# Ten unread TensorE products in the wait before the expert layer's first reload

## The chip, the cores and the metric

The kernel runs on one core of a Trainium2 chip. The metric is the device time of one execution in microseconds (us); lower is better. TensorE (PE) multiplies, VectorE (DVE) and ScalarE (ACT) do element-wise work, GpSimd (POOL) makes constants and scatters rows, and SyncE (SP) issues most DMAs. TensorE's clock has two levels here, 2.4 GHz (granted clock 1.00) and 1.2 GHz (0.50).

## The reference, cut to what matters

```python
def reference(x, ...):
    x = _L0_conv_ref(x, ...)           # group norm, deformable attention, GEGLU
    t = _to_tokens(x)                  # 4 x 256 tokens of 128
    t = t + _L1_attn_ref(_ln_t(t), ...)      # 8 heads of 16
    t = t + _L1_ffn_ref(_ln_t(t), ...)       # the stage around the change
    ...

def _L1_ffn_ref(hidden_states, gate_weight, w1, w2):   # 16 experts, top 2, F = 512
    x = hidden_states.reshape(-1, D)
    gate_logits = x @ gate_weight.T
    top_vals, top_idx = jax.lax.top_k(gate_logits, TOP_K)
    routing_w = jax.nn.softmax(top_vals, axis=-1)
    mask = jnp.any(top_idx[:, :, None] == jnp.arange(E)[None, None, :], axis=1)
    h = jax.nn.silu(jnp.einsum('td,efd->tef', x, w1))
    h_mean = jnp.einsum('tef,te->ef', h, mask) / jnp.maximum(counts, 1)[:, None]
    y_mean = jnp.einsum('ef,edf->ed', h_mean, w2)
    return jnp.einsum('tk,tkd->td', routing_w, y_mean[top_idx])
```

Each expert's hidden rows are averaged over the tokens that chose it; a token gets the weighted averages of its two experts.

## The kernel before, in words

Each engine has one instruction stream, and semaphores order them. The stage around the change is the expert layer.

The 1024 tokens are handled in two halves of 512. For each half DVE ranks the logits and computes a slot number for each (token, expert) pair, so that slots of one expert are together in rows of 32. POOL scatters the normalised rows `nrm` into a DRAM table of slots by eight indirect DMAs a half (line 509; semaphore `scattered[h]`). SP reads the table back in six groups of four slot tiles, 128 slots each (line 418, `reloaded[g]`, into the tile that the trace calls late). Groups 0 to 2 come from the first half, 3 to 5 from the second.

On PE each group g is turned to columns (`turn_slots`, line 1680, waits for `reloaded[g]`), and ACT copies the result out of PSUM (`columns_out`, line 776, `cols_ready`). Then `expert_tiles(g)` multiplies four tiles (lines 1697 and 1705) with w1 in fp32. A tile has four quarters of 32 slots, each with its own expert: the first reads w1 in place (`arena`), the other three read copies staged in one of 16 buffers. The first six copies are made by ACT (line 759, `staged_first`), all others by DVE (line 1199, `staged`), in the order of the tiles; from the 17th copy on a buffer is used again, and the copy waits for the tile that read it (`h_mm`). ACT applies Silu to each finished tile (line 786), waits for `h_mm` and gives `h_ready`; tile t writes PSUM bank 2 + t % 4, so tile 4 waits for the Silu of tile 0. `expert_sums` (line 1720) sums the hidden rows by expert. The order on PE is: turn groups 0 and 1, then for each g the tiles of g, the turn of g + 2, and the sums of g - 1. Later PE multiplies by w2 (line 1760), whose load SP issues after the reloads (line 423).

Before all this PE ranks the second half (`rank(1)`) and turns the residual stream (`turn_x2`, line 1602). Then it waits for the first reload. Meanwhile ACT normalises the second half, copies x2 out, makes copies 2 to 5 of the staged weights and an exponential, and DVE finishes the slots of the second half (line 1123), makes copies 6 to 11, and writes the routing table (line 1225, `route_ready`).

`keep_clock(n, bank)` (line 1385) issues n bf16 products of 128 x 128 by 128 x 512 of two constants, `ident_b` and `ones_b`, into a PSUM bank. It is already used in four places earlier in the kernel.

Of the kernel before, what the change touches and what calls it, by code (L numbers as in the profile page):

```python
# [48 lines left out]
FIRST_STAGED = 6  # L49
# [21 lines left out]
def build(nc, x, weights, vectors, rows, w1_t, w2_t, out):  # L71
    with ExitStack() as ctx:
# [216 lines left out]
        def sems(names):  # L289
            return [sem(n) for n in names.split()]  # L290
# [37 lines left out]
        lg_mm, gap_ready, e2_ready, route_ready, rt_mm, route_t_ready = sems(  # L328
            "lg_mm gap_ready e2_ready route_ready rt_mm route_t_ready")
        chosen_ready, rank_mm, slots_ready, experts_ready, slot_expert_ready, inv_quad_ready = sems(  # L330
            "chosen_ready rank_mm slots_ready experts_ready slot_expert_ready inv_quad_ready")
        cols_mm, cols_ready, staged_first, staged, h_mm, h_ready, sum_mm, h_rows_ready, fold_mm, hmean_ready = sems(
            "cols_mm cols_ready staged_first staged h_mm h_ready sum_mm h_rows_ready fold_mm hmean_ready")
# [44 lines left out]
        def slots_bank(g):  # L378
            return ps[:, (6, 1)[g % 2], :]
# [881 lines left out]
        def _(pe):  # L1261
# [123 lines left out]
            def keep_clock(n, bank):  # L1385

                for _ in range(n):
                    nc.tensor.matmul(ps[:, bank, :], ident_b[:, :], ones_b[:, :].unsqueeze(1).to_broadcast([P, 4, P]))
# [209 lines left out]
            def turn_x2(h):  # L1598

                pe.wait_ge(x2_ready, 2)  # L1600
                for t in range(4 * h, 4 * h + 4):
                    nc.tensor.transpose(slots_bank(h)[:, P * (t % 4):P * (t % 4) + P], x2_k[:, t, :], ident[:, :]).then_inc(x2_mm, 1)
# [67 lines left out]
            rank(1)  # L1670
            turn_x2(0)
            turn_x2(1)

            def turn_slots(g):

                pe.wait_ge(reloaded[g], 16)
                if g >= 2:
                    pe.wait_ge(cols_ready, g - 1)
                for j in range(GROUP):
                    nc.tensor.transpose(slots_bank(g)[:, j * P:(j + 1) * P], x_slots[:, GROUP * g + j, :],  # L1680
                                        ident[:, :]).then_inc(cols_mm, 1)
# [132 lines left out]
```

## Time and profile before

| | us |
|---|---|
| median of 3 runs | 275.45 (275.06 to 275.71) |
| the profiled execution, its own time | 275.87 |
| its span, first to last instruction | 273.9 |
| PE busy | 222.5 (81%) |
| DVE busy | 207.4 (76%) |
| ACT busy | 174.7 (64%) |
| mean granted TensorE clock | 0.944 |

Busy time is a sum over the whole span; the waits and the granted clock differ from stage to stage. All positions in the rows below are us from the start of the span.

### The profile page before, as it was taken

The numbers are of one execution on the slowest core, as the hardware profiler recorded it, in microseconds if no ns is written. First come the engines' busy times: TensorE is split into PE (matmuls) and PEld (weight loads), VectorE is DVE, ScalarE is ACT, GpSimd is POOL, SyncE is SP. The second block draws the span as 40 slices with busy tenths as digits, with TensorE's granted clock in tenths as the row PEclk, the third lists the DMA queues.
The fourth block names the chain that finished last, engine by engine and source line by source line (L and its number), as shares of the span: only waits on it lengthen the run. The fifth ranks groups of instructions, "written<-read, shape, count | busy, mean of one in ns | idle before, by whom it ended". The sixth has DMA issues, their size and how long they took to land.

```text
span 273.9 us, 7291 instructions
## 1 busy us (share of the span) xinstructions
PE 222.5 (81%) x2936; PEld 154.9 (57%) x2936; DVE 207.4 (76%) x482; ACT 174.7 (64%) x257; POOL 48.1 (18%) x64
## 2 busy tenths in 40 slices
PE   0799449999999998869999887889987307899985
PEld 0579327666767667637979755566556203233354
DVE  5766888999999999865335967888849957598412
ACT  5366898999999996066442567675667391565610
POOL 7004918910000000010001100000000677100000
PEclk9999859999999999997999999999999855999999
DMA  6930000000000000790000000000000115594002
GB/s 148 357 140 2 0 0 4 2 5 2 2 5 2 2 2 5 243 370 2 0 0 4 0 0 2 0 2 0 2 1 4 38 50 162 153 425 175 0 2 77
DMA packets 8590, 16.38 MB, mean 60 GB/s; under 512 B 752, under 2 KB 5104, under 8 KB 8304
## 3 DMA queue, kind: packets, MB, share of 16 engines
q1 hardware_dynamic: 8048, 14.90, 15.5%
q0 software_dynamic: 512, 1.05, 1.2%
q8 instruction: 23, 0.38, 0.6%
q14 instruction: 7, 0.06, 0.1%
HBM read 12.80 MB, written 3.15 MB: 58 GB/s over the span
## 4 chain that ended last, share of the span: by engine, by line
issue 54%; PE 30%; DVE 8%; ACT 3%; DMA 3%; SPq 1%; DVEq 1%; ACTq 0%
PE ps L1697 8%; PE ps L1380 6%; DVE wide L991 5%; PE ps L1720 2%; DVE msda L996 2%; DMA r_sb<-in_rows 2%; ACT arena L594 1%; PE ps L1760 1%; PE ps L1282 1%; PE ps L1680 1%; PE ps L1366 1%; PE ps L1335 1%; DMA late<-slot_rows 1%; PE ps L1311 1%; PE ps L1323 1%
## 5 line engine op out<-in xcount | busy, mean ns | idle before, releaser
L594 ACT ACTIVATE arena<-ps,one_less_sq 128x1024 bf16<-128x1024 f32 x64 | 67.2, 1112 | 4.7 <-PE ps L1366 4.7
L1380 PEld LDWEIGHTS ps<-arena 128*128 128x128 bf16 x1536 | 43.3, 96 | 19.8 <-issue 10.4
L1380 PE MATMUL ps<-arena 128*128 128x48 bf16 x1536 | 49.4, 184 | 5.1 <-DVE wide L991 4.6
L996 DVE TENSOR_REDUCE msda<-wide 128x768 f32 x32 | 46.1, 1513 | 0.0
L1366 PE MATMUL ps<-wide,sel 64*128 64x512 bf16 x128 | 25.7, 400 | 7.3 <-ACT arena L594 7.3
L991 DVE TENSOR_TENSOR wide<-ps,wide 128x768 f32<-128x768 f32 x32 | 30.1, 1009 | 1.1 <-PE ps L1380 1.1
L509 POOL DMA_INDIRECT slot_rows<-nrm,slots x16 | 16.1, 1006 | 66.2 <-ACT nrm L732 61.7
L1697 PE MATMUL ps<-arena,w_sb 128*32 x48 | 23.5, 636 | 1.0 <-ACT sel L786 1.0
L1046 DVE TENSOR_REDUCE t_k<-ps 128x2 f32<-128x512 f32 x32 | 20.5, 684 | 0.0
L668 ACT ACTIVATE wide<-ps 128x512 f32<-128x512 f32 x32 | 17.3, 594 | 1.4 <-PE ps L1526 1.3
L1705 PE MATMUL ps<-late,w_sb 128*32 128x512 f32 x80 | 16.6, 667 | 0.0
L1199 DVE COPY late<-arena 128x512 f32 x34 | 12.0, 423 | 4.8 <-PE ps L1705 3.0
L1021 DVE SCALAR_TENSOR_TENSOR wide<-ps,v_sb,wide 128x512 f32<-128x512 f32 x8 | 5.9, 750 | 11.8 <-ACT wide L640 9.2
L1039 DVE SCALAR_TENSOR_TENSOR xm<-ps,raw_by,xm 128x512 fp32r<-128x512 f32 x16 | 11.9, 748 | 3.7 <-ACT xm L657 1.9
L1697 PEld LDWEIGHTS ps<-arena,w_sb 128*32 128x32 f32 x48 | 5.4, 117 | 16.3 <-issue 16.3
L786 ACT ACTIVATE sel<-ps 128x512 f32<-128x512 f32 x12 | 6.9, 601 | 9.7 <-PE ps L1705 9.7
L1680 PE MATMUL ps<-ident,late 128*128 128x128 f32 x24 | 4.5, 330 | 10.1 <-DMA late<-slot_rows 10.1
L1366 PEld LDWEIGHTS ps<-wide,sel 64*128 64x128 bf16 x128 | 6.2, 93 | 11.1 <-ACT arena L594 7.7
L660 ACT ACTIVATE xm<-ps,high_by 128x512 fp32r<-128x512 f32 x8 | 5.5, 686 | 10.5 <-PE ps L1488 10.5
L495 POOL MEMSET t_k<- 128x1024 f32 x1 | 1.0, 952 | 63.4 <-PE ps L1426 63.4
L640 ACT ACTIVATE wide<-ps,v_sb 128x512 f32<-128x512 f32 x8 | 5.4, 694 | 9.6 <-PE ps L1444 9.6
L1680 PEld LDWEIGHTS ps<-ident,late 128*128 128x128 f32 x24 | 3.2, 166 | 13.0 <-issue 13.0
(320 smaller groups left out, 510.7 us busy)
## 6 DMA issues: line engine op xcount, KB each, us to landing
arena<-in_w_t SPq DMA_DIRECT2D x1, 4096.0 KB, 13.6
wide<-in_w_t SPq DMA_DIRECT2D x1, 4096.0 KB, 15.2
w_sb<-in_weights SPq DMA_DIRECT2D x1, 1544.0 KB, 8.8
slot_rows<-t_c SPq DMA_DIRECT2D x2, 768.0 KB, 10.4
late<-slot_rows SPq DMA_DIRECT2D x6, 256.0 KB, 3.3
x_sb<-in_x SPq DMA_DIRECT2D x4, 128.0 KB, 2.3
out<-xn SPq DMA_DIRECT2D x4, 128.0 KB, 1.8
r_sb<-in_rows SPq DMA_DIRECT2D x1, 288.0 KB, 4.7
```

Of the source, the lines that this page charges most:

```text
L509: nc.gpsimd.indirect_dma_start(out=scratch[h], out_offset=bass.IndirectOffsetOnAxis(ap=slots[:, c, t:t + 1], axis=0), in_=nrm[:, t, :], in ...
L594: nc.scalar.activation(hot[:, u, c:c + 5:4, :, :], ps[:, 2 * (c % 2):2 * (c % 2) + 2, :].rearrange("r p (b q) -> r p b q", b=B), ACT.Relu, ...
L668: nc.scalar.activation(prob_t[u % 2][:, i, :], ps[:, 2 + i % 2, :], ACT.Exp).then_inc(prob_ready, 1)
L991: nc.vector.tensor_tensor(prod[:, c, :, :, :], g, w.unsqueeze(3).to_broadcast([P, 2, NP * NK, DH]), ALU.mult).then_inc(g_free, 1)
L996: nc.vector.tensor_reduce(msda[:, 4 * c + u:4 * c + u + 3:2, bass.ds(i, 1), :].rearrange("q b h d -> q b (h d)"), prod[:, c, :, :, :].rear ...
L1039: nc.vector.scalar_tensor_tensor(out=to, in0=ps[:, 6 + of_keys, :].rearrange("c (n t) -> c n t", n=2), scalar=raw_by[:, of_keys:of_keys + ...
L1046: nc.vector.tensor_reduce(nmax[:, :, 2 * (u % 2) + i // 2, HROWS * (i % 2) + SPLIT], ps[:, i % 2, :].rearrange("q (t k) -> q t k", t=2), A ...
L1199: nc.vector.tensor_copy(staged_at[n % len(staged_at)], w1_sb[:, bass.ds(at[q][t % GROUP], 1), :].rearrange("d e f -> d (e f)")).then_inc(s ...
L1366: ins = nc.tensor.matmul(ps[:, 2 * (c % 2) + a, :], sel[rows, i % 4, c, :], terms_t[rows, i // 4, u * HALF:(u + 1) * HALF])
L1380: ins = nc.tensor.matmul(ps[:, 4 + b, p * NK * DH:(p + 1) * NK * DH], hot[:, u, p, b, :], rhs, start=(s == 0), stop=(s == PARTS - 1))
L1697: nc.tensor.matmul(ps[0:GRAIN, 2 + t % 4, :], x_cols[:, t * P:t * P + GRAIN], w1_sb[:, bass.ds(at[j], 1), :].rearrange("d e f -> d (e f)"))
L1705: ins = nc.tensor.matmul(ps[GRAIN * q:GRAIN * (q + 1), 2 + t % 4, :], x_cols[:, t * P + GRAIN * q:t * P + GRAIN * (q + 1)], staged_at[entr ...
```

## The change

After the second call of `turn_x2` PE waits for ACT's six staged weight copies, issues eight `keep_clock` products into PSUM bank 2, waits for the routing table, and issues two more. Nothing reads their result; tile 0 overwrites the bank.

```diff
             turn_x2(0)
             turn_x2(1)
+            pe.wait_ge(staged_first, FIRST_STAGED)
+            keep_clock(8, 2)
+            pe.wait_ge(route_ready, 1)
+            keep_clock(2, 2)
```

`FIRST_STAGED` is 6. The instructions that follow are unchanged: a wait for ACT's copies of x2 and `turn_slots(0)`.

## Rows read from the trace of the kernel before

**Rows 1.** The page's 40 equal slices: TensorE's granted clock in tenths.

```profile
PEclk9999859999999999997999999999999855999999
```

**Rows 2.** Stretches: busy us (instructions) of PE, PEld, DVE, ACT, POOL; clock; DMA.

```profile
122.00:124.00 2.00, 1.19 (x4) 0.75 (x5) 1.27 (x5) 1.98 (x4) 0.00 (x0) 1.00 0.47 173
124.00:126.00 2.00, 2.00 (x10) 1.61 (x9) 1.69 (x4) 0.90 (x2) 0.00 (x0) 0.58 0.00 0
...
216.00:218.00 2.00, 1.66 (x8) 1.26 (x8) 1.86 (x12) 0.67 (x2) 1.59 (x2) 0.62 0.21 66
218.00:223.00 5.00, 0.00 (x0) 0.00 (x0) 3.07 (x13) 4.68 (x10) 3.78 (x5) 0.50 0.17 54
...
227.80:229.70 1.90, 1.86 (x8) 1.51 (x8) 1.69 (x10) 0.60 (x1) 1.60 (x2) 0.50 0.82 256
...
232.00:234.00 2.00, 2.00 (x16) 0.52 (x12) 1.16 (x4) 0.00 (x0) 1.68 (x2) 0.62 0.11 33
```

**Rows 3.** The chain that ended last: start, duration, what.

```profile
224.85 2.78 DMA late<-slot_rows
...
227.84 1.94 PE ps L1680 x8
```

**Rows 4.** Timeline of PE, 215 to 241: start, duration, what, idle time before.

```profile
216.09 1.66 PE L1602 MATMUL ps<-ident,t_k 128*128 128x128 f32 x8 [0.28 <-DVE t_k L1072]
...
229.72 1.06 PE L1697 MATMUL ps<-arena,w_sb 128*32 x1
...
235.16 0.66 PE L1680 MATMUL ps<-ident,late 128*128 128x128 f32 x4
236.86 0.61 PE L1697 MATMUL ps<-arena,w_sb 128*32 x1 [1.05 <-ACT sel L786]
...
240.43 0.66 PE L1680 MATMUL ps<-ident,late 128*128 128x128 f32 x4
```

**Rows 5.** Timeline of ACT, 220 to 238.

```profile
220.83 2.18 ACT L759 ACTIVATE late<-arena 128x512 f32 x4
...
228.97 0.60 ACT L776 ACTIVATE w_sb<-ps 128x512 f32<-128x512 f32 x1 [2.93 <-PE ps L1680]
...
236.02 2.07 ACT L786 ACTIVATE sel<-ps 128x512 f32<-128x512 f32 x4 [5.60 <-PE ps L1705]
```

**Rows 6.** Timeline of DVE, 221 to 239.

```profile
222.25 0.74 DVE L1199 COPY xn<-arena 128x512 f32 x2
...
225.66 0.37 DVE L1225 TENSOR_TENSOR x_sb<-picked_w 128x128 f32<-128x128 f32 x1
...
231.72 0.76 DVE L1199 COPY t_k<-arena 128x512 f32 x2 [1.46 <-issue]
...
236.12 2.78 DVE L1199 COPY late<-arena 128x512 f32 x8 [2.96 <-PE ps L1705]
```

**Rows 7.** Timeline of PE, products of 512 columns, in two places.

```profile
126.42 0.63 PE L1444 MATMUL ps<-xm 128*128 128x512 f32 x1
126.84 0.63 PE L1441 MATMUL ps<-xm 128*128 128x512 f32 x1
...
157.56 1.04 PE L1388 MATMUL ps<-ones_b,ident_b 128*128 128x512 bf16 x4
```

**Rows 8.** SP's issue of the fourth reload, and DMA issues by line (KB, us to landing).

```profile
235.27 0.36 SPq L418 DMA_DIRECT2D late<-slot_rows  x1
...
late<-slot_rows SPq DMA_DIRECT2D x1, 256.0 KB, 2.9
...
wide<-in_w_t SPq DMA_DIRECT2D x1, 4096.0 KB, 15.2
```

**Rows 9.** Timeline of POOL, 222 to 234.

```profile
222.41 1.08 POOL L509 DMA_INDIRECT slot_rows<-nrm,slots  x1 [0.31 <-issue]
223.79 0.96 POOL L509 DMA_INDIRECT slot_rows<-nrm,slots  x1 [0.30 <-issue]
...
232.91 1.08 POOL L509 DMA_INDIRECT slot_rows<-nrm,slots  x1 [0.30 <-issue]
```

## Prediction

> **What bounds the kernel now.** I read the page's slices first, then the stretches, the chain, and the timelines of four engines around the edit. PE is busy most of the span, and the clock row has one long low place, slices 32 to 34 [rows 1]. The stretches give its edges: the granted clock falls while PE turns the last x2 tiles (0.62 in 216 to 218), is 0.50, that is 1.2 GHz, through the idle stretch (0.00 us busy from 218 to 223) and through PE's first work after it, and is back at 1.00 (2.4 GHz) before 234 [rows 2]. At 0.62 over 232 to 234, 1.52 us of those two were at half, so the clock rose at about 233.5, 5.7 us after PE had started again at 227.84.
>
> In the chain the reload of the scattered rows ends the wait (2.78 us from 224.85), and PE's work follows from 227.84 on [rows 3]. So everything PE does from 227.84 sets the end. In the timeline [rows 4] tiles 0 to 3 take 229.72 to 235.16, 5.44 us, where tiles 4 to 7 at the full clock take 236.86 to 240.43, 3.57 us. Between the two PE waits 1.05 us for ACT: the first Silu starts only at 236.02, though tile 0 was issued at 229.72 [rows 5], and DVE's copy into the re-used staging buffer, which waits for the same tile, starts at 236.12 [rows 6]. Both were held back by tile 0's completion. I don't know why it came so late (two passes at half clock end near 231.5); it matters below.
>
> **The fillers.** Nothing is removed. PE gains two waits and ten products, all in its wait from 216.09 + 1.66 = 217.75 to 227.84 [rows 4]. Eight start when ACT's sixth weight copy is done, 220.83 + 2.18 = 223.01 [rows 5]. No row shows such a product at the low clock. The nearest are 512-column products of the same shape in the other low stretch, 126.42 to 126.84: 0.42 us apiece [rows 7]. At the full clock four such products took 1.04 with their tail, so 0.26 each at most [rows 7]. Bounds for the eight: 2.1 us (all full) to 5.0 us (0.63 each, the whole duration of a record at half). I take 3.4 us, since back-to-back products pace by the start-to-start time: they end at 226.4. The route table is written at 225.66 + 0.37 = 226.03 [rows 6], so the other two follow without a wait: at 0.42 each they end at 227.3, at 0.26 at 226.9. The reload lets PE go at 227.84: 0.5 us of slack. They cost nothing because this DMA wait hides them; behind them on PE stands only the first turn of the slots. They write PSUM bank 2, which by the code no engine reads until tile 0 has written it, and read two constants. If the cover were gone, 3.4 + 0.85 = 4.3 us would be the price.
>
> **What the clock gives back.** PE will have worked 3.7 to 4.3 us without a pause before 227.3, where it now has to work 5.7 us from 227.84. I expect the rise by about 227 to 229. In steps:
> - Slots 0 to 7 are turned in 1.94 us at half [rows 3]; four at full take 0.66 [rows 4]. ACT's first copy starts 1.13 after the turns start (228.97) [rows 5]; it will start at 227.84 + 0.68 = 228.52. Tile 0 comes 0.75 after that copy's start (229.72 against 228.97), so at 229.27: 0.45 gained.
> - Tiles 0 to 3 take 3.57 instead of 5.44: the third turn starts at 232.84 instead of 235.16, 2.3 gained.
> - Tile 0 is complete near 230.4, its Silu (0.6) near 231.0, long before tile 4 wants the bank. The 1.05 wait goes: with 0.66 for four turns tile 4 starts at about 233.5 instead of 236.86, 3.35 gained.
> - DVE: its first four new copies start at 231.72 whatever PE does (four at 0.35 each, to 233.1), then it goes on at 2.78/8 = 0.35 each [rows 6] instead of waiting for 236.12. Tile 7's last copy, the eighth after these, is there at 233.1 + 2.8 = 235.9; tile 7 wants it at 233.5 + 3 x 0.89 = 236.2. Just in time. Tile 7 ends at 237.1.
>
> **What is late next: the fourth reload.** After tile 7 PE turns slots 12 to 15, which come from the second half's scatter. SP issues that reload at 235.27 and it lands 2.9 later, 238.17 [rows 8]; with the 0.21 that PE needed after the first landing (227.84 against 224.85 + 2.78 = 227.63 [rows 3]) the turns start at 238.38. They start at 240.43 now [rows 4]. So 3.35 shrinks to 2.05, and PE waits 1.3 us anew. One term more: the scatter itself is a row of POOL instructions, 0.96 + 0.30 = 1.26 apart, but 1.38 from 222.41 to 223.79, where DVE copied weights at the same time [rows 6, 9]. DVE's copies now also run under the last one, 232.91 to 233.99. Between 0 and 0.3 us (two or three such delays); I take 0.1, as most of the last ones already lie beside copies. Nothing else is moved. After 240.43 PE's work stays as it is: 3.57 for four tiles and 0.66 for a turn [rows 4], and the sums on top. DVE makes a tile's three copies in 1.05 us, against 0.89 for the tile alone and 1.06 with its share of the turn, and is by then further ahead than now. The w2 load is issued after the reloads (at 236 to 237) and lands 15.2 later, about 252 [rows 8]; PE asks for it after four more groups, not before 240.4 + 4 x 4.2 = 257, or 255.
>
> Sum: 2.05 - 0.1 = 1.95. The profiled execution took 275.87 for a span of 273.9 (1.97 around it), so 273.9 for the new one. The median of the runs, 275.45, is 0.42 lower. Where in such a wait the clock rises need not repeat, so some plain runs may have lost less; the new time doesn't hang on it, since a rise as late as 230 is still hidden in the 1.3 us wait. I put the new median 0.3 lower than the new profiled time: **273.6**.
>
> **A rule that speaks against it.** In this trace PE's first 1.9 us after the wait were turns, at 0.50 throughout [rows 2, 3], which doesn't say whether turns count for the clock. The Trainium skill ("TensorE: Matmul & The Clock Gate", Part 4: PE-mode transpose) says that the full clock doesn't engage for transposes, which don't count as busy in the same way. By that rule the clock would see nothing from 227.3 to 229.3 after the fillers; if that cost the rise, the time would be that of the rival "nothing comes of it".
>
> **Rivals.**
> 1. *Nothing comes of it* (0.13). Tile 0's completion came at 236.0, and both its readers agree [rows 5, 6]. If it was held by something with its own time (the last scatter, POOL to 233.99 [rows 9], and its writes), tile 4 stays at 236.86 however fast tiles 0 to 3 are, and the time is 275.45. So too if the fillers don't raise the clock, or if the rise is lost during the turns (0.04 of the 0.13). Against it: the turns just before, also at half clock, were answered promptly (ACT at 228.97 [rows 5]), and what sets tiles 0 to 3 apart from the later ones is the low clock.
> 2. *Part is given back* (0.13). The new 1.3 us wait before the fourth reload may let the clock fall. From 122 to 124 PE was busy 1.19 of 2.00 us and the clock was half soon after: 0.58 over the next two [rows 2], 1.7 us of them at half, and still half at 126.84 [rows 7]. I take twice that, 3.4 us, as such a stretch; it costs up to 1.7 us: 273.6 + 1.7 = 275.3 at worst, 274.8 when part of it falls in waits. PE's work around the new wait is denser than it was there.
> 3. *Slower* (0.06). The fillers overrun the reload. If each takes 0.63 at half [rows 7], ten end at 223.0 + 6.3 = 229.3, the turns start 1.5 late, and without an early rise nothing pays for it: 275.45 + 1.5 = 276.9. This decides from 0.46 us each on (227.6 - 223.0 over ten); the start-to-start rows say 0.42, so the margin is thin, but an overrun with a risen clock still gains.
> 4. *More than forecast* (0.02): the runs' fourth reload earlier than in the profile; 272.8.
>
> **The numbers.** The forecast holds 0.66, from 273.0 (no loss in the scatter and 0.4 of scatter in the runs) to 274.2. Under 0.2% (0.55 us) no change can be told. Rival 1 lies inside it, rival 2 mostly outside on the fast side (0.11 of 0.13): faster 0.79, same 0.15, slower 0.06. The range takes the forecast and most of rival 2: 272.9 to 275.0.
>
> **What would show it.** After: clock row 1.00 from about 227 to 229 on; ten products at the fillers' line from 223.0 to about 227.1; turns still at 227.84; tile 0 near 229.3; first Silu near 230.4; tile 4 near 233.5; a new PE wait of 1 to 1.4 us that a DMA ends at about 238.4. Wrong if the first Silu stays at 236, if the turns start after 228, or if the clock row shows a second low place at 236 to 242.

## The result, and the profile after

The changed kernel took 278.0 us (median of 5 runs, 277.53 to 279.76) against 275.45 (5 runs, 275.06 to 279.5) for the kernel before on the same chip. The ratio is 1.0094, with a 95% interval from 1.0048 to 1.0141: slower by about 1%, where faster was forecast. Medians and ranges, here and below, are over all runs, while each ratio is taken over the fast ones alone (the 279.5 is a slow one), so it is not the quotient of the medians. The profiled execution took 277.53 us for a span of 275.5, so its span is 1.6 longer than the one the prediction was made against.

First the page's row of the granted clock and five stretches (columns as in [rows 2]) of the changed kernel:

```profile
PEclk9999858999999999997999999999999757799999
```

```profile
226.00:228.00 2.00, 1.48 (x5) 0.29 (x4) 1.84 (x8) 0.30 (x2) 1.46 (x2) 0.74 0.83 245
228.00:230.00 2.00, 1.29 (x8) 0.83 (x8) 1.76 (x9) 0.00 (x0) 1.62 (x2) 1.00 0.79 246
230.00:232.00 2.00, 0.50 (x4) 0.20 (x8) 0.42 (x2) 0.60 (x1) 1.39 (x3) 0.61 0.11 33
232.00:234.00 2.00, 2.00 (x12) 0.41 (x8) 1.34 (x4) 0.00 (x0) 1.69 (x2) 0.50 0.21 66
...
236.00:238.00 2.00, 2.00 (x13) 0.42 (x7) 1.26 (x4) 1.49 (x4) 0.00 (x0) 0.68 0.58 170
```

The clock rises at about 227.04 (0.74 over 226 to 228 leaves 0.96 us at full), is 1.00 while the slots are turned, and falls again at about 230.45 (0.61 over 230 to 232), to come back at about 237.3. PE was busy only 0.50 of 230 to 232. Its timeline says why (L1684 is the turns, L1701 and L1709 the tiles; the four new lines stand ahead of them):

```profile
223.33 4.15 PE L1388 MATMUL ps<-ones_b,ident_b 128*128 128x512 bf16 x10 [5.37 <-issue]
228.02 0.63 PE L1684 MATMUL ps<-ident,late 128*128 128x128 f32 x4 [0.54 <-DMA late<-slot_rows]
228.92 0.66 PE L1684 MATMUL ps<-ident,late 128*128 128x128 f32 x4 [0.28 <-DMA late<-slot_rows]
231.50 1.05 PE L1701 MATMUL ps<-arena,w_sb 128*32 x1 [1.93 <-issue]
...
237.92 0.66 PE L1684 MATMUL ps<-ident,late 128*128 128x128 f32 x4
238.50 0.62 PE L1701 MATMUL ps<-arena,w_sb 128*32 x1
...
242.08 0.66 PE L1684 MATMUL ps<-ident,late 128*128 128x128 f32 x4
```

The ten products end at 227.48, before the reload. The turns are over at 229.58, sooner than before. But tile 0 waits another 1.93 us, which [rows 4] had not. It needs ACT's copy of the turned columns, and ACT's timeline has it late:

```profile
230.77 0.60 ACT L776 ACTIVATE w_sb<-ps 128x512 f32<-128x512 f32 x1 [4.46 <-PE ps L1684]
236.51 0.60 ACT L776 ACTIVATE w_sb<-ps 128x512 f32<-128x512 f32 x1 [5.15 <-remote]
237.01 2.06 ACT L786 ACTIVATE sel<-ps 128x512 f32<-128x512 f32 x4
```

The first four turns ended at 228.65, and ACT, which had nothing to do, copies only at 230.77: 2.1 us late. The second four ended at 229.58, and their copy comes at 236.51, 6.9 us late. Before, the first copy came 1.13 us after the turns' start and only the first Silu was late [rows 5]. So what was late behind tile 0 before is late two steps sooner now: a wait that a reader finds in ACT's rows and not in PE's. DVE's timeline has the same hold in its second row here, which needs tile 0; the first waits 0.81 us for a signal of DVE's own:

```profile
230.75 0.20 DVE L1237 TENSOR_SCALAR in_quad<-quad_i 128x64 f32<-128x64 int32 x1 [0.81 <-DVE inv_cnt L1236]
...
236.74 2.78 DVE L1199 COPY late<-arena 128x512 f32 x8 [2.64 <-remote]
```

And what happens beside it, on POOL the last scatter, on SP the fourth reload, which waits for the scatter to have landed:

```profile
233.12 1.13 POOL L509 DMA_INDIRECT slot_rows<-nrm,slots  x1 [0.31 <-issue]
```

```profile
235.55 0.36 SPq L418 DMA_DIRECT2D late<-slot_rows  x1
```

**Where the time went.** This execution is 0.28 us behind the earlier one already before the edit (first scatter at 213.59 for 213.32), which isn't of the change. With that taken off, tile 0 is 1.50 late (231.50 - 0.28 against 229.72). Tiles 0 to 3 up to the third turn take 6.42 instead of 5.44, as they run at half nearly to the end: 0.98 more. The 1.05 wait before tile 4 is gone, with 0.07 around it (0.58 from third turn to tile 4, for 1.70): 1.12 back. 1.50 + 0.98 - 1.12 + 0.28 = 1.64, and the fourth turn is at 242.08 for 240.43. From there on nothing differs: the span is 1.6 longer.

### The profile page after: what moved, and what is told of

The parts are those of the page before. It is cut to its first block, busy times and chain, and to the rows that moved or that the text cites. A ratio compares the mean times of both kernels' runs of the same rounds, so it can differ in the third digit from the quotient of the medians.

```text
span 275.5 us, 7311 instructions
## 1 busy us (share of the span) xinstructions
PE 227.1 (82%) x2946; PEld 155.8 (57%) x2946; DVE 207.3 (75%) x482; ACT 174.8 (63%) x257; POOL 48.1 (17%) x64
## 3 DMA queue, kind: packets, MB, share of 16 engines
q0 software_dynamic: 512, 1.05, 1.2%
## 4 chain that ended last, share of the span: by engine, by line
PE 52%; issue 16%; DVE 15%; ACT 8%; DMA 4%; POOL 2%; DVEq 1%; SPq 1%; ACTq 0%; POOLq 0%
PE ps L1701 8%; DVE wide L991 5%; PE ps L1380 5%; DVE t_k L1046 4%; PE ps L1488 3%; PE ps L1454 3%; DVE msda L996 3%; POOL slot_rows L509 2%; PE ps L1541 2%; PE ps L1724 2%; PE ps L1502 2%; PE ps L1266 2%; DMA r_sb<-in_rows 2%; PE ps L1514 2%; PE ps L1444 2%
## 5 line engine op out<-in xcount | busy, mean ns | idle before, releaser
L1701 PE MATMUL ps<-arena,w_sb 128*32 x48 | 24.5, 658 | 1.9 <-issue 1.9
L1709 PE MATMUL ps<-late,w_sb 128*32 128x512 f32 x80 | 17.3, 686 | 0.0
L1701 PEld LDWEIGHTS ps<-arena,w_sb 128*32 128x32 f32 x48 | 5.6, 119 | 17.0 <-issue 17.0
L1388 PE MATMUL ps<-ones_b,ident_b 128*128 128x512 bf16 x22 | 7.4, 479 | 5.4 <-issue 5.4
L1488 PE MATMUL ps<-z_h,wqk_h 128*128 128x256 f32 x32 | 10.4, 325 | 0.0
L776 ACT ACTIVATE w_sb<-ps 128x512 f32<-128x512 f32 x6 | 3.6, 605 | 10.0 <-remote 5.1
```

The source lines that it names most:

```text
L1488: ins = nc.tensor.matmul(ps[:, 6 + of_keys, j * HW:(j + 1) * HW], w[:, at_w:at_w + P], z[:, b * HW:(b + 1) * HW], start=(n == 0), stop=(n ...
L1701: nc.tensor.matmul(ps[0:GRAIN, 2 + t % 4, :], x_cols[:, t * P:t * P + GRAIN], w1_sb[:, bass.ds(at[j], 1), :].rearrange("d e f -> d (e f)"))
L1709: ins = nc.tensor.matmul(ps[GRAIN * q:GRAIN * (q + 1), 2 + t % 4, :], x_cols[:, t * P + GRAIN * q:t * P + GRAIN * (q + 1)], staged_at[entr ...
```

## The experiments

Each group ran on one chip beside runs of the kernel before. Medians of that kernel were 276.23 (35 runs), 276.52 (25), 277.52 (7), 276.14 (31) and 276.6 (17) in the five groups, with single runs from 274.84 to 280.98; ratios are against that kernel in the same group, with a 95% interval. "Copies" are ACT's two copies of the turned columns, "answered" means that ACT starts 0.7 to 1.2 us after the turns' start.

### The change and its parts

**The changed kernel once more.**

> The changed kernel once more, for its spread and a second trace. Theory A (late completions): in the changed kernel's trace the signal that PE has turned the first four slot tiles reaches ACT at 230.77, 2.1 us after the turns ended, so tile 0 starts at 231.50; this should come again, 277.5 to 279.8 us, first ACT copy of columns near 230.7. Theory B (an accident of the phase of the clock in that run): the first ACT copy near 228.6 in this trace and a time near 275.

277.47 us, 1.0034 [1.0008, 1.0061]; span 276.0. Turns at 229.07, copies at 231.75 and 237.47, first Silu at 237.96, clock up at 228.45 and down at 231.86. The loss repeats on another chip in the same places, at about 1 us instead of 2.5. DVE's wait for itself repeats too (0.82 us before the same instruction).

**The two waits without the products.**

```
             pe.wait_ge(staged_first, FIRST_STAGED)
-            keep_clock(8, 2)
             pe.wait_ge(route_ready, 1)
-            keep_clock(2, 2)
```

> The two waits alone, no products. Both theories: nothing, 275.4 plus or minus 0.5, because the waits end at 226 and the reload ends PE's wait at 227.8. If the waits themselves do harm (rival C), it is slower by over 1 us, as the changed kernel.

276.38, 1.0005 [0.9977, 1.0033]. Copies at 229.35 and 230.34 after turns at 228.22, first Silu at 236.48, as before. The waits cost nothing.

**Only the eight.**

```
             pe.wait_ge(staged_first, FIRST_STAGED)
             keep_clock(8, 2)
-            pe.wait_ge(route_ready, 1)
-            keep_clock(2, 2)
```

> The first wait and its eight products, ending near 226.7, without the two behind the route table. Theory A with the harm from PE work right up to the reload: less harm than with ten, the columns' copy at 228.6 to 229.5, 274 to 276. Theory A with the harm from products in the wait as such, or from a clock that is at full when the turns come: as the changed kernel, 277.5 to 278.5. Clock theory (the clock rises and falls again because PE's work is thin after the products): 277 to 278, a second low place in the clock row.

275.81, 1.0021 [0.9991, 1.0051]; span 273.5. The fillers (222.38 to 225.97) are followed by 1.25 us of idling, and the clock rises at 231.28 only. ACT:

```profile
228.34 0.60 ACT L776 ACTIVATE w_sb<-ps 128x512 f32<-128x512 f32 x1 [2.98 <-issue]
233.36 0.60 ACT L776 ACTIVATE w_sb<-ps 128x512 f32<-128x512 f32 x1 [4.42 <-remote]
235.61 2.07 ACT L786 ACTIVATE sel<-ps 128x512 f32<-128x512 f32 x4 [1.66 <-PE ps L1707]
```

The first copy is answered 1.12 us after the turns' start, the second is 4 us late. Two products fewer have moved the first late answer by one step, and with tile 0 on time (229.13) no loss can be measured. By its interval it could still be up to 1.4 us, so it is the rows and not the time that set this kernel apart from the changed one. Nothing is gained either: the Silu still starts at 235.61, and PE stops inside tile 3:

```profile
234.76 0.59 PE L1707 MATMUL ps<-q_c,w_sb 128*32 128x512 f32 x1 [0.95 <-issue]
```

**Only the two.**

```
-            pe.wait_ge(staged_first, FIRST_STAGED)
-            keep_clock(8, 2)
             pe.wait_ge(route_ready, 1)
             keep_clock(2, 2)
```

> Only the second wait and its two products, 226.0 to 226.9. The clock cannot rise from 0.9 us of work, so PE stays at half until about 233.5. If the harm needs the clock to have risen: 275.4, nothing changes. If it comes from products shortly before the turns: 277 or more, with the columns' copy late by 1 to 2 us.

277.18, 1.0034 [1.0003, 1.0065]. Both copies are answered (230.08 and 230.94, turns at 228.96), the first Silu is at 237.43. In this profiled execution PE itself stopped between the four products of the third turn, 0.60 and 1.15 us, and the clock fell once more (238.67 to 242.09); its time, 278.98, is in the upper part of this kernel's runs (275.1 to 279.51). By the ratio two products lose as much as ten did in this group (1.0034 both times), though both copies are answered. So the times of this group don't rank the parts; what follows goes by the rows and by larger effects.

### Is it the clock, or the scatter?

My theory after these: while the indirect DMAs of the scatter run, PE's signals of completion are held. The rival: the loss is the second low place of the clock.

**A bridge of eight more products behind the second turn**, to keep the clock up over the new wait:

```
             turn_slots(0)
             turn_slots(1)
+            keep_clock(8, 2)
```

> The changed kernel with eight more products right behind the second turn, so that PE isn't idle while it waits for the copied columns. Clock theory (the loss is that the clock falls a second time at 230.5): one low place only, tiles 0 to 3 at full, 274.5 to 275.5. Completion theory (everything PE reports between 229 and 236 is held until the second half's scatter is over): tiles 0 to 3 run faster but the first Silu still comes near 237, so tile 4 stays near 238.5 and the time at 276.5 to 278.

277.13, 1.0011 [0.9965, 1.0057]; span 275.9. The clock row has no second low place, and tile 0 runs at full, yet PE stops in the second pass of tile 2 and goes on only at 235.75 and 236.47:

```profile
PEclk9999858999999999997999999999999559999999
```

```profile
231.60 0.61 PE L1701 MATMUL ps<-arena,w_sb 128*32 x1
...
235.75 0.59 PE L1709 MATMUL ps<-late,w_sb 128*32 128x512 f32 x1 [1.38 <-issue]
236.47 0.59 PE L1709 MATMUL ps<-xn,w_sb 128*32 128x512 f32 x1
...
238.86 0.62 PE L1701 MATMUL ps<-arena,w_sb 128*32 x1
```

Copies are at 230.86 and 236.50, first Silu at 237.00, tile 4 at 238.86 against 238.50 in the changed kernel. With the clock at full the second copy and the first Silu come where they came in the changed kernel (236.51 and 237.01), and tile 4 is no sooner: the late answers don't hang on the clock. For the price of the low clock this is no clean test, as the bridge issues eight more products, and PE stopped.

**Eight of the sixteen indirect DMAs left out**, from the kernel before and from the changed one (the second half's slots are not written, and the reloads no longer wait for them, so that SP issues the last reload and the load of w2 some 7 us sooner):

```
-            for t in range(TILES):
+            for t in range(4):
...
-                if n == 0:
-                    sp.wait_ge(scattered[h], 16 * 4 * TOPK)
+                if g == 0:
+                    sp.wait_ge(scattered[0], 16 * 4 * TOPK)
```

> The kernel before without the second half's eight scatters (its slots are then rows of zeros; SP doesn't wait for them). Completion theory: the first Silu comes about 231.7, right after tile 0, and the 1.05 us wait before tile 4 is gone: 1 us faster or a little more. Clock theory: first Silu still near 236, time within 0.5 us.

275.46, 0.9956 [0.9912, 1.0001], at the edge of the noise. The first Silu starts at 233.63, 2.0 us after tile 0 (231.63), instead of 6.3 after it.

> The changed kernel without the second half's eight scatters. Completion theory: the columns' first copy at 228.6, tile 0 at 229.3 to 229.5, first Silu near 230.4, tile 4 near 233.5 and, with no fourth reload to wait for, 2 to 3.5 us faster than the kernel before, which is what the change was worth without the hold. Clock theory: it still loses the clock at 230.5 and ends within 1 us of the changed kernel.

272.93 (4 runs), 0.9865 [0.979, 0.9941]. With all ten fillers in place every answer is prompt:

```profile
229.53 0.63 PE L1684 MATMUL ps<-ident,late 128*128 128x128 f32 x4 [0.45 <-DMA late<-slot_rows]
230.52 0.66 PE L1684 MATMUL ps<-ident,late 128*128 128x128 f32 x4 [0.36 <-DMA late<-slot_rows]
231.31 0.61 PE L1701 MATMUL ps<-arena,w_sb 128*32 x1
...
235.47 0.62 PE L1701 MATMUL ps<-arena,w_sb 128*32 x1
```

```profile
230.20 0.60 ACT L776 ACTIVATE w_sb<-ps 128x512 f32<-128x512 f32 x1 [2.58 <-PE ps L1684]
231.21 0.60 ACT L776 ACTIVATE w_sb<-ps 128x512 f32<-128x512 f32 x1 [0.41 <-PE ps L1684]
232.44 0.60 ACT L786 ACTIVATE sel<-ps 128x512 f32<-128x512 f32 x1 [0.63 <-PE ps L1709]
```

Here what I had predicted happens: tile 4 starts 5.94 us after the turns do (forecast: 233.5 - 227.84 = 5.66), at the full clock from 228.96 on. Against the kernel before without the same DMAs the fillers are worth about 2.5 us (272.93 against 275.46; the profiled spans, 272.5 and 274.5, say 2.0; ten and four runs, whose ranges overlap). They work, where the scatter doesn't run beside them.

**Half of the second half's indirect DMAs** (one in place of two for each of its tiles), in the changed kernel:

```
-                for c in range(TOPK):
+                for c in range(TOPK if h == 0 else 1):
```

> The changed kernel with four of the second half's eight scatters (second choices left out), so that POOL ends about 5 us earlier, near 229.2. Completion theory: the hold ends about 5 us earlier, near 231.5, first Silu by 232, and the time falls to 274 or less. Clock theory: first Silu at 236 to 237 as before, unchanged time.

274.34, 0.9886 [0.9837, 0.9934]. The last one now ends on POOL at 229.15 instead of 234.25, and the fourth reload is issued at 230.83. The copies (229.41 and 230.93, after turns at 228.29 and 229.72) and the first Silu (232.51, 2.0 behind tile 0) are answered: the first copy 1.4 us and the Silu 4.5 us sooner than in the changed kernel, with the scatter over 5.1 sooner. Here SP still waits for the second half. The clock fell in this run too, at about 230.6 (0.64 over 230 to 232), and came back at 234.0, with prompt answers throughout: the second low place of the clock doesn't need the hold.

**POOL as busy as before, but not with DMAs:** in the changed kernel each of those eight is replaced by two memsets of POOL.

```
+                if h == 1:
+                    for c in range(TOPK):
+                        nc.gpsimd.memset(y_rest[:, :, :], 0.0)
+                        nc.gpsimd.memset(y_pos[:, :, :], 0.0).then_inc(pool_step, 1)
+                        pool.wait_ge(pool_step, 5 + 2 * (t - 4) + c)
+                    continue
```

> The changed kernel with the second half's eight scatters replaced by sixteen memsets of about the same total time on POOL. If POOL being busy is what holds PE's answers, it is as the changed kernel. If it is the indirect DMAs themselves: prompt answers and 272.5 to 273.5, as without them.

274.84, 0.9892 [0.9827, 0.9957], a median above the 272.5 to 273.5 expected, on a chip on which the kernel before is slower too (277.52). POOL has rows of this kind in place of the scatter's, and ACT's lines have nothing late (lines stand 6 further on):

```profile
224.82 0.70 POOL L510 MEMSET y_rest<- 128x512 f32 x1
```

```profile
229.91 0.60 ACT L782 ACTIVATE w_sb<-ps 128x512 f32<-128x512 f32 x1 [2.56 <-PE ps L1690]
231.26 0.60 ACT L782 ACTIVATE w_sb<-ps 128x512 f32<-128x512 f32 x1 [0.75 <-PE ps L1690]
232.49 0.60 ACT L792 ACTIVATE sel<-ps 128x512 f32<-128x512 f32 x1 [0.63 <-PE ps L1715]
```

A busy POOL isn't it. What is left is the indirect DMAs, or what went out with them here and in the two runs above: SP's long wait for their last signal. No run has the DMAs without that wait.

### What of the fillers uses it up: their time or their number?

**Twenty products of 16 columns** in the place of the ten of 512:

```
+            def tiny(n):
+                for _ in range(n):
+                    nc.tensor.matmul(ps[:, 2, 0:16], ident_b[:, :], ones_b[:, 0:16])
...
             pe.wait_ge(staged_first, FIRST_STAGED)
-            keep_clock(8, 2)
-            pe.wait_ge(route_ready, 1)
-            keep_clock(2, 2)
+            tiny(20)
```

> Twenty products of 16 columns at the place of the fillers (some 1.3 us of PE, no rise of the clock, done by 225). Budget theory: while the scatters run, about twelve products since PE's last long pause are answered promptly and what comes after is held until the scatters end, whatever the products' length. Then even the first turns' answers are late: first columns copy at 230.5 or later, tile 0 near 231.5, 276.5 to 278.5 us, as the changed kernel. Clock or PE-time theory: nothing happens, 275.4 to 276.2 as the kernel before, first columns copy 1.1 us after the turns start.

282.87 (281.88 to 283.95), 1.0204 [1.0136, 1.0271]: some 5.4 us slower, from 0.70 us of work that lies in a wait, where 1 to 3 were expected.

```profile
223.00 0.70 PE L1675 MATMUL ps<-ones_b,ident_b 128*128 128x16 bf16 x20 [5.38 <-issue]
227.82 1.94 PE L1686 MATMUL ps<-ident,late 128*128 128x128 f32 x8 [4.11 <-DMA late<-slot_rows]
237.13 1.05 PE L1703 MATMUL ps<-arena,w_sb 128*32 x1 [7.38 <-ACT w_sb L776]
```

```profile
236.40 1.09 ACT L776 ACTIVATE w_sb<-ps 128x512 f32<-128x512 f32 x2 [10.41 <-remote]
239.13 0.60 ACT L786 ACTIVATE sel<-ps 128x512 f32<-128x512 f32 x1 [1.64 <-PE ps L1711]
```

Turns on time at 227.82, and not one of their answers before 236.4. The number of products (each with its weight load) does it, not their time, and not a fall of the clock, which is at half from before the products until past 240.

**The same twenty 4 us earlier**, right behind the x2 turns (219.25 to 219.98), to see whether a pause restores what they use up:

> The same twenty small products right behind turn_x2, at 217.8, 9 us before the turns. Budget theory with a budget that recovers in a pause: no harm, as the kernel before. Budget theory without recovery: as the changed kernel, 276.5 to 278.5. Clock theory: no change.

282.95, 1.0189 [1.0113, 1.0266]. PE then rests 9.21 us, turns at 229.19, and both copies come at 237.83. A pause restores nothing while the scatter runs. DVE is held here as well, at signals of its own (each of its short steps waits for the one before):

```profile
230.53 0.56 DVE L1181 TENSOR_TENSOR t_k<-expert_of,expert_f 128x384 f32<-128x384 f32 x1 [1.04 <-DVE expert_of L1180]
...
232.66 0.18 DVE L1234 TENSOR_TENSOR cnt<-cnt,cnt_half 128x16 f32<-128x16 f32 x1 [1.28 <-issue]
233.38 0.17 DVE L1235 TENSOR_SCALAR cnt<-cnt 128x16 f32<-128x16 f32 x1 [0.55 <-DVE cnt L1234]
```

From 229 to 236 such gaps are 4.2 us in this run, 4.0 in the run with sixteen below (2.03 the longest) and 1.5 in the one with twenty above. The kernel before and the runs without the second half's DMAs have none.

**Sixteen products of 256 columns** in the fillers' place:

> Sixteen products of 256 columns in place of eight of 512: the same PE time as in the run with eight (whose first columns copy was prompt and the second held), double the count. Budget theory: the first columns copy is held too, by about 2 us or more, and the time is 1 to 2 us over that run with eight products. Time theory: like the run with eight.

282.71, 1.0174 [1.0105, 1.0243]. PE works 3.60 us in the fillers' place, as the eight of 512 did in 3.59, and loses what the twenty small ones lose (copies at 238.13, tile 0 at 238.86 after turns at 229.53). That is 5 us, where 1 to 2 more than with the eight were expected.

**Four, eight and twelve of 16 columns**, and **twenty of them ahead of the last outputs' turn**, so that they are over before the first indirect DMA is issued:

> Four products of 16 columns at the fillers' place. Counted from the first scatter there are 14 before (6 of the ranking, 8 turns of x2), so the last of the 8 slot turns is number 26. In the run with eight fillers number 26 was answered promptly and the next were held. If the count decides: both columns copies prompt (1.1 and 2 us after the turns start), first Silu held until about 1 us after the fourth reload's issue, as in the kernel before; time as before.

> Eight small products: the fourth slot turn is number 26, the eighth number 30. Count: first columns copy prompt, the second held to 233 or later, tile 0 on time; time within 1 us of the kernel before.

> Twelve small products: the fourth turn is number 30. Count: the first columns copy is held by 2 us or more, up to the end of the scatters, and the time is 1.5 to 5 us over the kernel before, though PE's added work is 0.4 us in a 10 us wait.

> Twenty small products before the last output turns, near 209, some 4 us ahead of the first scatter. If the scatters open the count: prompt columns copies and the time of the kernel before plus at most 0.7 us for the products themselves, which lie on the path there. If every product counts, wherever it is: columns copy held to the end of the scatters, 281 to 284.

These came out at 276.23, 0.9994 [0.9956, 1.0033]; 276.63, 1.0004 [0.9957, 1.0051]; 278.08, 1.0036 [0.9987, 1.0084]; and 277.05, 1.0026 [0.9991, 1.0062]. No ratio is clear of noise, not even that of twelve, whose median is 1.9 us up; ACT's rows tell them apart. Counted are PE's products from the first indirect DMA on: 6 that rank the pairs (215.5), 8 turns of x2, the fillers, and the turns of the slots up to the fourth and the eighth.

| kernel | fillers | count at 4th turn | its copy | count at 8th turn | its copy |
|---|---|---|---|---|---|
| before | 0 | 18 | answered | 22 | answered |
| only the two | 2 | 20 | answered | 24 | answered |
| four small | 4 | 22 | answered | 26 | answered |
| only the eight | 8 | 26 | answered | 30 | 4.2 late |
| eight small | 8 | 26 | answered | 30 | 2.0 late |
| changed | 10 | 28 | 2.1 late | 32 | 6.9 late |
| changed, once more | 10 | 28 | 2.0 late | 32 | 6.9 late |
| twelve small | 12 | 30 | 2.6 late | 34 | 6.1 late |
| sixteen of 256 columns | 16 | 34 | 7.5 late | 38 | right behind it |
| twenty small | 20 | 38 | 7.5 late | 42 | right behind it |
| twenty small, 4 us earlier | 20 | 38 | 7.5 late | 42 | right behind it |
| twenty ahead of the scatter | 0 | 18 | answered | 22 | answered |

("Late" is against the answered rows: at half clock 1.13 us after the turns' start, and 0.85 behind the first copy; in the changed kernel, at full, 0.67 after the start of each four, as in the run without the second half's DMAs.) Big or small, eight fillers leave the fourth turn answered and the eighth not:

```profile
228.64 0.60 ACT L776 ACTIVATE w_sb<-ps 128x512 f32<-128x512 f32 x1 [2.93 <-PE ps L1686]
231.45 0.60 ACT L776 ACTIVATE w_sb<-ps 128x512 f32<-128x512 f32 x1 [2.21 <-remote]
235.80 2.07 ACT L786 ACTIVATE sel<-ps 128x512 f32<-128x512 f32 x4 [3.75 <-PE ps L1711]
```

So some 26 products are answered at once after the scatter begins, the next few come through late, and the rest when the scatter has landed. Counted from the start of the first DMA the late copies stand in few places: at 17.1 to 17.2 us in the three executions with ten fillers, at 18.5 with eight and with twelve small ones, at 20.7 with the eight big ones, and at 22.8 to 23.1 in all other cases; the last DMA starts at 19.5 to 19.6 in these.

The number is good to a few products only. Where PE ran at half before the scatter, some products of the last projection start after the first DMA too: three with only the eight (up to 0.6 us after it), five with sixteen, with twenty 4 us earlier and with twenty ahead of the scatter (up to 1.0 us). With these, only the eight had product 29 answered, where 28 was late in the changed kernel. Either the count opens a microsecond after the first DMA's start, or it isn't a plain count.

**A test of that number.** If it were simply 26, tile 0's completion, the 30th in the kernel before, would be answered at once with four products fewer. In the kernel before, the turn of the first four x2 tiles was put ahead of the last projection, with the two PSUM banks of the turns swapped and its wait cut to the half that it needs:

```
+            turn_x2(0)
             project_out(1)
...
-            turn_x2(0)
             turn_x2(1)
```

> The kernel before with the first four x2 turns moved ahead of the second half's output projection, before the first scatter (they take PSUM bank 1, the last four bank 6). Nothing is added. Counted from the first scatter tile 0 is then number 26 instead of 30. Count reading: first Silu some 2 us after tile 0's start (near 231.7 to 232.5) instead of 236, the 1.05 us wait before tile 4 gone, 0.5 to 1.2 us faster than the kernel before. If the hold comes by time (whatever PE reports after 231 is held): first Silu at 236, no change.

277.0, 0.9992 [0.9949, 1.0035]. Missed: the first Silu is held as ever.

```profile
229.28 0.60 ACT L776 ACTIVATE w_sb<-ps 128x512 f32<-128x512 f32 x1 [3.13 <-PE ps L1680]
230.13 0.60 ACT L776 ACTIVATE w_sb<-ps 128x512 f32<-128x512 f32 x1 [0.26 <-issue]
236.37 2.07 ACT L786 ACTIVATE sel<-ps 128x512 f32<-128x512 f32 x4 [5.64 <-PE ps L1705]
```

The number holds for the fillers and turns that it was read from. It doesn't carry to a tile, whose products go to four column groups with weights for each, or to products moved so close to the scatter's start.

None of the versions with the whole computation in it was measurably faster than the kernel before.

## Why the prediction was wrong

**The step that failed.** "ACT's first copy starts 1.13 after the turns start (228.97); it will start at 227.84 + 0.68 = 228.52. Tile 0 comes 0.75 after that copy's start, so at 229.27: 0.45 gained." It took for granted that PE's completion would be answered as promptly as before. It came at 230.77, and tile 0 at 231.50. Everything behind it (3.35 gained at tile 4, the third turn at 232.84, the new wait before the fourth reload) fell with that, and so did "They cost nothing because this DMA wait hides them": the wait hides their time, but not their number.

**Point by point.**
- The fillers' length: forecast 3.4 + 0.85 = 4.3 us, measured 4.15, over at 227.48. They delayed no turn: 228.02 is 0.18 later in an execution that was 0.28 behind already. Right.
- The clock's rise at 227 to 229: 227.04. Right. That it might be lost again stood in rival 2, at the fourth reload; it was lost seven microseconds earlier, at 230.45, in the wait for ACT.
- The tiles at full 3.57 us, tile 4 at 233.5: without the second half's scatter the trace has the pattern, 5.94 us from turns to tile 4 against 5.66. In the changed kernel as it is, tile 4 is at 238.50. The gain is real, but the scatter takes it.
- The fourth reload as the next bound, and DVE's copies under it: never reached.
- Rival 1 named the right thing, "held by something with its own time (the last scatter [...])", and gave it 0.13 and a time of 275.45. What I held against it, that the turns just before were answered promptly [rows 5], was true of 22 products and not of 32. I asked whether the fillers help against the hold, and not whether they feed it. The slower rival, an overrun of the reload, didn't happen.
- The unexplained row was the warning: "I don't know why it came so late". A late signal whose cause isn't known lay on the path, and the sum treated it as if it were the clock's.

**The size.** The profile accounts for 1.64 us, 1.36 of it from the change. The ratio of the first runs, 1.0094, is 2.6 us [1.3 to 3.9], that of the repeat on another chip 0.9 [0.2 to 1.7]. Both hold about 1.4. Of that, 1.50 is the late first answer, 0.98 the half clock on tiles 0 to 3, and 1.12 comes back as the wait before tile 4 goes. Not all of the 0.98 is the clock's to give back: the first Silu at 237.01 would have let tile 4 start at about 237.85 (0.84 behind it, as 236.86 to 236.02 before) instead of 238.50, so by this estimate at most 0.65. In the bridge, with the clock up, PE stopped in tile 2 instead.

**What is shown and what isn't.** Shown: the hold comes with the indirect DMAs (without half of them no answer is late, with memsets in their place neither, and it ends with them), and products issued after the first of them bring it on by their number (0.70 us of work cost 5.4), with no recovery over 9 us. It isn't PE's alone. DVE waited for signals of its own too: 0.81 and 0.82 us in the two executions of the changed kernel, 0.4 in the bridge, 0.5 and 0.7 with only the eight and only the two, 1.5 in all with twenty small products. PE also stopped by itself for 0.60 to 1.38 us, inside a tile in the bridge and with only the eight, inside a turn with only the two and with eight small ones. Neither is in the kernel before or in the runs without the second half's DMAs. That these are the same hold is likely from where they occur, but no run separates them.

Open: what holds the signals, how a tile counts, and whether SP's wait for the scatter has a part in it. Open too is whether the hold is there in an execution that isn't recorded. All runs here were recorded with a row for each instruction, and a hold that goes by the number of instructions and not by their time is also what one would see if writing these records were what backs up beside the DMAs. No run rules that out; the times themselves (5.4 us) come from recorded executions as well.

The Trainium skill ("TensorE: Matmul & The Clock Gate", Part 3, The cost: per-tile semaphore tail) says that increments at completion are written one after another, about 26 ns each: 0.5 us for sixteen. The answers here are 2 to 7.5 us late for eight turns and prompt without the scatter, so that tail isn't what these rows show.

The rule of the Trainium skill that I had weighed ("TensorE: Matmul & The Clock Gate", Part 4: PE-mode transpose), that turns in transpose mode don't count for the clock, stays open: the slots' turns ran at 1.00 right behind the fillers, and the clock fell at 230.45, when PE had turned and then stood still since 229.58; with ordinary products in that gap (the bridge) it stayed up. No run parts the turns from the standstill.

## What to carry to other kernels

Work put into a wait can cost more than its time. Where indirect DMAs run beside it, count the products, and keep the unread ones few and long (eight of 512 columns cost nothing that could be measured, sixteen of 256 cost 5 us, in recorded executions). Before trusting that a change is hidden, put twenty of the smallest instruction of that kind in its place: if the time moves, something other than the engine's time is being used up. And where a row shows an engine idle beside finished input, as ACT's first Silu was here, find what holds it (leave out the neighbour that ends at the same time) before pricing anything that lies ahead of it.

## What the runs showed that I had not expected

- Twenty matrix products of 16 columns, 0.70 us of PE in a 10 us wait, made the kernel 5.4 us slower (1.0204 [1.0136, 1.0271]).
- During 16 indirect DMAs, one each 1.26 us, PE's first 26 or so products were answered within 1.2 us, the next ones 2 to 4 us late, and the rest after the last had landed, up to 7.5 us late (twenty small: due at 227.82 + 1.13 = 228.95, there at 236.40). With eight of those DMAs fewer all are prompt.
- PE itself stopped in such a stretch, in the middle of a tile, for 1.38 us, and DVE waited up to 2.03 us at a time between short instructions of its own (sixteen of 256 columns).
- The clock rose after 3.7 us of products of 512 columns (223.33 to 227.04) and fell 3.4 us later, PE having stood for the last 0.9 of it.
